# Convolution in half units at both ends of a MetaFormer kernel, with the first image's FFN spread over the second unit

## What is computed

```python
x = x + conv(ln_c(x)) + ln_c(x)        # depthwise 3x3, SAME, per channel
t = to_tokens(x)                       # (32, 112*112, 96)
h = relu(qlinear(ln_t(t), W1, b1))     # q_mul: float8 e5m2 of both operands
t = t + qlinear(h, W2, b2)             # q_acc: float16 of the sums
x = from_tokens(t)
```

## Time and profile before

| | us |
|---|---|
| median of 3 runs | 3290.78 |
| lowest, highest | 3288.11, 3294.91 |
| the profiled execution | 3289.0 |
| its span on the core (first to last instruction) | 3287.3 |

### The profile page before, as it was taken

The page is one execution under the profiler, slowest core; times in us unless marked ns, Lnnn a source line. Parts: engine busy times, 40 slices in busy tenths (PEclk is TensorE's granted clock), DMA queues, the critical chain, the costliest instruction groups (busy, mean ns, idle before and its releaser), DMA issues.

```text
span 3287.3 us, 78227 instructions
## 1 busy us (share of the span) xinstructions
PE 2986.9 (91%) x24902; PEld 2502.7 (76%) x24902; DVE 3161.5 (96%) x11557; ACT 3068.9 (93%) x7282; POOL 1922.4 (58%) x913
## 2 busy tenths in 40 slices
PE   5689999999999999999999999999999999999876
PEld 5577777777877777787777778777777877788644
DVE  8559999999999999999999999999999999999998
ACT  7779999999999999999999999999999999986666
POOL 0005666666666666666666666666666666666676
PEclk9999999999999999999999999999999999999966
DMA  7777777787777777777777778777777877766533
GB/s 222 213 206 218 226 228 226 229 232 224 232 226 229 226 229 232 225 230 228 228 226 229 232 223 231 228 228 224 231 231 225 230 227 229 226 199 179 158 118 102
DMA packets 277434, 713.58 MB, mean 217 GB/s; under 512 B 35001, under 2 KB 35106, under 8 KB 277026
## 3 DMA queue, kind: packets, MB, share of 16 engines
q1 hardware_dynamic: 271394, 694.12, 72.6%
q10 hardware_dynamic: 5632, 14.45, 1.3%
HBM read 539.84 MB, written 168.59 MB: 216 GB/s over the span
## 4 chain that ended last, share of the span: by engine, by line
DVE 52%; ACT 23%; PE 18%; issue 5%; DMA 2%; POOL 1%; DVEq 0%; SPq 0%; POOLq 0%; ACTq 0%
DVE stats L650 16%; DVE xq L687 14%; PE conv_ps L430 11%; ACT images L522 10%; DVE hid L640 9%; ACT hid L502 7%; DVE hid L645 6%; PE hid_ps L393 3%; PE y_ps L408 3%; ACT images L533 2%; DVE images L699 2%; ACT y L510 2%; DVE y L667 2%; DVE rstd L678 1%; DVE xt_ps L674 1%
## 5 line engine op out<-in xcount | busy, mean ns | idle before, releaser
L430 PE MATMUL conv_ps<-images,band_ring 112*112 112x222 f32 (+1 forms) x8928 | 1872.8, 354 | 30.2 <-DMA band_ring<-bands 29.5
L430 PEld LDWEIGHTS conv_ps<-images,band_ring 112*112 112x112 f32 x8928 | 1545.6, 177 | 177.9 <-issue 31.5
L275 POOL TENSOR_TENSOR xf<-xf,y 112x768 f32<-112x768 f32 x448 | 953.0, 2127 | 1101.1 <-DVE y L667 1101.1
L502 ACT ACTIVATE hid<-hid_ps 128x896 f16<-128x896 f32 x1344 | 1234.1, 931 | 89.6 <-PE hid_ps L393 89.6
L270 POOL TENSOR_TENSOR xf<-xf,images 112x768 f32<-112x768 f32 x448 | 982.2, 2192 | 259.7 <-ACT images L533 246.4
L522 ACT ACTIVATE images<-xn,neg_mean,rstd 112x96 f32<-112x96 f32 x2800 | 1088.1, 561 | 15.8 <-DVE neg_mean L682 11.3
L408 PEld LDWEIGHTS y_ps<-w2t,hid 128*128 128x128 f16 x10752 | 584.8, 100 | 365.8 <-ACT hid L502 194.4
L408 PE MATMUL y_ps<-w2t,hid 128*128 128x96 f16 x10752 | 668.3, 210 | 190.1 <-ACT hid L502 159.9
L687 DVE SCALAR_TENSOR_TENSOR xq<-xf,stats,xt_ps 112x96 fp8e5<-112x96 f32 x3584 | 840.5, 310 | 0.0
L393 PE MATMUL hid_ps<-xt,w1t 96*128 96x448 fp8e5 x2688 | 681.0, 363 | 16.9 <-ACT xt L494 16.9
L640 DVE TENSOR_SCALAR hid<-hid,b1q 128x896 f16<-128x896 f16 x1344 | 583.9, 466 | 12.8 <-ACT hid L502 12.3
(11 more groups left out here) (54 smaller groups left out, 763.5 us busy)
## 6 DMA issues: line engine op xcount, KB each, us to landing
band_ring<-bands SPq DMA_DIRECT2D x744, 294.0 KB, 5.1
xf<-in_x SPq DMA_DIRECT2D x462, 336.0 KB, 5.1
out<-xf SPq DMA_DIRECT2D x448, 336.0 KB, 3.9
xn<-in_x SPq DMA_DIRECT2D x434, 336.0 KB, 3.4
bands<-images ACTq DMA_DIRECT2D x16, 882.0 KB, 7.8
xf<-bands SPq DMA_DIRECT2D x24, 294.0 KB, 4.3
xf<-in_L_ffn_W SPq DMA_DIRECT2D x2, 144.0 KB, 2.8
xf<-in_L_conv_kernel SPq DMA_DIRECT2D x3, 3.4 KB
```

Source lines behind the costliest of these rows:

```text
L275: pool.tensor_tensor(res, res, y[:, e % 2], ALU.add).then_inc(summed, CW)
L430: mm = pe.matmul(dst[:, :, lo:hi], band_place(t < CONV_AT + UNIT, n)[:, PAIR * dx + i, :], images[:, m % 2, :, ch, lo + dx - 1:hi + dx - 1 ...
L502: nc.scalar.activation(hid[:, e % 2, TOK * j:TOK * (j + 1)].rearrange("p (u n) -> p u n", u=2), hid_ps[:, k, :, 0:HALF * H], ACT.Identity) ...
```

## The change

There are 17 units in place of 16: the first has image 0 alone and the last image 31 alone ("half units"), those between have images 1 and 2, 3 and 4, and so on. A half unit goes through the same 96 channels in the same 28 steps, with matmuls of 112 (or 111) moving columns in place of 224, and saves half as much for each group. Convolution begins at t = -43 (`CONV_AT`), 15 steps after the first normalisation in place of 29, and ends at t = 432.

The FFN of image 0 (chunks 0 to 13) is done in the steps -14, -12, ..., 12, during the convolution of unit 1 (images 1 and 2); from t = 14 chunk t is done in step t as before.

The banded matrices are built in three thirds of 84 larger builds, six in each step, into three separate images of the buffer `images`, in the order third 2, 0, 1. Unit 0 takes thirds 0 and 1 as weights right from where they were built and loads only third 2 (16 groups); its ring of six is gone. A normalisation that writes over a third waits until it was sent and used (`STAGED_AT`).

The first 42 chunks take moments, roots and reciprocals one step earlier (`early`), and have the ring of four and 5 columns on ACT. DVE's moments no longer wait for ACT's normalisation two chunks before; the reciprocal does.

On PE the waits of `ffn1` stand at `ffn1` itself, one for each third, no longer ahead of the matmul before it; the second third no longer waits for the first cast of its own chunk. The diff, cut to its core (that `r` and `c` are gone from all functions, with the loop that was not in use, is left out):

```diff
-FIRST_BAND_RING = 6
...
+        THIRDS = 3
+        STAGES = [(1, 1), (0, 0), (1, 0)]
+        BUILT = (2, 0, 1)
+        STAGED_AT = {CHUNKS: 2, 2 * CHUNKS: 0, 3 * CHUNKS: 1}
+        TGROUPS = GROUPS // THIRDS
+        QB = NB // THIRDS
+        def band_stage(q):
+            b, i = STAGES[q]
+            return images[:, b, i, :, :].rearrange("p c w -> p (c w)")[:, 0:QB * H] \
+                .rearrange("p (g n h) -> p g n h", g=TGROUPS, h=H)
...
+        SEND_AT = {2: (4, 1), 0: (14, 2), 1: (22, 2)}
+        STEP_SETUPS = 6
...
-        CONV_AT = -UNIT - 1
+        CONV_AT = -UNIT - 1 - CHUNKS
+        UNITS = B // IMGS + 1
+        FIRST_NORMS = UNIT + CHUNKS
...
+        def ffn(t):
+            if t < CHUNKS:
+                return [(t + CHUNKS) // 2] if t >= -CHUNKS and t % 2 == 0 else []
+            return [t] if t < TOTAL else []
...
+        def unit_images(t):
+            m = (t - CONV_AT) // UNIT
+            return slice(1, IMGS) if m == 0 else slice(0, 1) if m == UNITS - 1 else slice(0, IMGS)
...
-            return (e // UNIT) % 2, e // CHUNKS % IMGS, slice(CW * k, CW * k + CW)
+            return (e + CHUNKS) // UNIT % 2, (e // CHUNKS + 1) % IMGS, slice(CW * k, CW * k + CW)
...
+        def early(t, lag):
+            late, soon = t + lag + LOOP, t + lag + LOOP + 1
+            return [n for n in (late, soon) if 0 <= n < TOTAL and (n == soon) == (n < FIRST_NORMS)]
...
+        LOADED_FROM = 2 * TGROUPS
+        def bands_at(n):
+            if n < LOADED_FROM:
+                return band_stage(n // TGROUPS)[:, n % TGROUPS]
+            return band_ring[:, (n - LOADED_FROM) % BAND_RING]
...
-                    if e % UNIT == 0:
-                        wait(pool, conv_saved, GROUPS * (2 * r + e // UNIT + 1))
+                    if e == 0 or (e + CHUNKS) % UNIT == 0:
+                        wait(pool, conv_saved, GROUPS * ((e + CHUNKS) // UNIT + 1))
...
-                def ffn1_may_start(r, e):
-                    wait(pe, xt_copied, LOOP * r + e + 1)
-                    wait(pe, hid_cast, J * (LOOP * r + e))
-                def ffn1_may_end(r, e):
-                    wait(pe, hid_cast, J * (LOOP * r + e) + J - 2)
...
+                def ffn1(e, j):
                     k = (J * e + j) % 2
+                    if j == 0:
+                        wait(pe, xt_copied, e + 1)
+                    wait(pe, hid_cast, J * e + j - 1)
...
-                            if w == HALF - 1 and j == J - 1 and at_last:
-                                at_last()
...
-                        mm = pe.matmul(dst[:, :, lo:hi], band_place(t < CONV_AT + UNIT, n)[:, PAIR * dx + i, :],
-                                       images[:, m % 2, :, ch, lo + dx - 1:hi + dx - 1], start=(dx == 1),
+                        mm = pe.matmul(dst[:, imgs, lo:hi], bands_at(n)[:, PAIR * dx + i, :],
+                                       images[:, m % 2, imgs, ch, lo + dx - 1:hi + dx - 1], start=(dx == 1),
...
-                    for s in normed:
-                        wait(dve, s, LOOP * r + n - 1)
+                    wait(dve, normed[1], n - 1)
...
                 def invert_c(n):
+                    wait(dve, normed[0], n - 1)
```

More of the change, by code:

```diff
@@ L227, in setups, with band_arrival @@
+        def band_arrival(n):
+            return band_in[(n - LOADED_FROM) % BAND_RING], dma_count(n - LOADED_FROM, BAND_RING)
+        def setups(t):
             n = STEP_SETUPS * (t - NORM_AT)
-            return range(n, min(n + STEP_SETUPS, QUARTERS * SETUPS)) if c == t and n >= 0 else range(0)
+            return range(n, min(n + STEP_SETUPS, THIRDS * SETUPS)) if n >= 0 else range(0)
         def run(eng, step):
-            for c in range(NORM_AT - 1, LOOP_AT):
-                step(0, c, c)
@@ L233, in run @@
[L233 to L238, removed]
+            for t in range(NORM_AT - 2, END):
+                step(t)
         with nc.Block() as block:
@@ L306, in store, with load_xf @@
[L306 to L310, removed]
+                    return dram[n, :, cols, :]
+                def load_xf(e):
+                    sp.dma_start(xf[0:H, e % FFN_RING], chunk_of(x, e)).then_inc(xf_in[e % FFN_RING], 16)
+                def store(e):
+                    wait(sp, summed, CW * (e + 1))
+                    sp.dma_start(chunk_of(out, e), xf[0:H, e % FFN_RING]).then_inc(x_out[e % FFN_RING], 16)
@@ L311, in load_xn, with load_bands @@
+                def load_xn(n):
                     for s in normed:
-                        wait(sp, s, norm_place_free(r, n))
-                    sp.dma_start(norm_place(n), chunk_of(x, r, n)).then_inc(norm_arrival(r, n)[0], 16)
-                def load_bands(r, c, t):
+                        wait(sp, s, norm_place_free(n))
+                    sp.dma_start(norm_place(n), chunk_of(x, n)).then_inc(norm_arrival(n)[0], 16)
+                def load_bands(t):
                     for ch in conv_channels(t):
[L317 to L325, removed]
@@ L341, in _, with step @@
+                def step(t):
+                    for n in early(t, 3):
+                        load_xn(n)
+                    for e in ffn(t + 3):
+                        wait(sp, x_out[(e) % FFN_RING], dma_count(e - FFN_RING, FFN_RING))
+                    for e in ffn(t - 3):
+                        store(e)
+                    for e in ffn(t + 3):
+                        load_xf(e)
+                    load_bands(t + 2)
                 run(sp, step)
                 for i in range(FFN_RING):
-                    sp.wait_ge(x_out[i], dma_count(0, TOTAL - 1 - (TOTAL - 1 - i) % FFN_RING, FFN_RING))
+                    sp.wait_ge(x_out[i], dma_count(TOTAL - 1 - (TOTAL - 1 - i) % FFN_RING, FFN_RING))
@@ L491, in copy_xt @@
-                def copy_xt(r, e):
-                    wait(act, xt_mm, LOOP * r + e + 1)
+                            act.wait_ge(s, SETUPS // 2 * (BUILT.index(third) + 1))
+                    lo, hi = TGROUPS * k // SENDS, TGROUPS * (k + 1) // SENDS
+                    act.dma_start(bands[TGROUPS * third + lo:TGROUPS * third + hi].rearrange("g h n k -> h g n k"),
+                                  band_stage(third)[:, lo:hi]).then_inc(bands_out[third], 16)
+                def copy_xt(e):
+                    wait(act, xt_mm, e + 1)
@@ L574, in step @@
-                    if ffn_in(t - 1):
-                        cast_hid(r, c - 1, 1)
-                    if norm_in(t + 2):
-                        root_c(r, c + 2 + LOOP)
-                    if ffn_in(t - 1):
-                        cast_hid(r, c - 1, 2)
+                    for third, (at, every) in SEND_AT.items():
+                        k, off = divmod(t - NORM_AT - at, every)
+                        if 0 <= k < SENDS and off == 0:
+                            send(third, k)
+                    for e in ffn(t - 1):
+                        cast_hid(e, 2)
```

388 lines of the change are left out of this document (168 added, 220 removed).

## The result

| | before | after |
|---|---|---|
| median, us | 3289.45 (4 runs) | 3265.75 (4 runs) |
| lowest, highest | 3286.89, 3294.91 | 3262.9, 3270.03 |
| span of the profiled execution | 3287.3 | 3264.0 |

The ratio is 0.9927 with a 95% interval from 0.991 to 0.9944; a second set of six runs of the changed kernel gave 3267.43 us and 0.9933 (0.992 to 0.9945). The forecast was 3270 us, with a sum of 3266.3 for the span.

A forecast was written before the change was run, and what follows sets the result against it. VectorE was taken to set the full stage's pace. Head 327 + full steps 2578.7 + 93.5 + 164 + 103.1 = 3266.3 us of span, 21 under 3287.3, so 3270 us forecast; own range 3254 to 3285, overall 3238 to 3306.

The forecast's parts named there:

- Part 1: Setup until the first convolution: 3.79 us a step in place of 3.29, convolution starting at 72 us (64 to 80).
- Part 2: First half unit with normalisation, 28 steps: 3.4 us each, 95 us (80 to 120).
- Part 3: Full convolution, normalisation and every other FFN step before t = 14: TensorE leads, 29 steps of 5.5, 160 us (151 to 180).
- Part 4: Full steps: 377 at an unchanged 6.840 us, 2578.7 us, only the edited waits acting here.
- Cost and gain zero: Full steps: ffn1's changed waits free TensorE, which has spare time, so 0 us, hidden by VectorE's 100%.
- Part 5: Tail: 14 last-convolution steps at 6.68, 93.5 us; then 28 steps of FFN with half a convolution at 5.85, 164 us.
- the stall: FFN steps of the tail: add_bias slowed beside POOL's addition, 0.6 us a step; without it 5.24, 17 us less.
- A: Rival: TensorE's clock falls in the tail, mean step 7.53, +47 us, 3317 us; chance 0.13.
- C: Rival: ffn1's waits at its weight loads lift TensorE's full step to 6.96, +45 us, 3315 us; chance 0.06.
- B: Rival: the head doesn't fill, 4.0 us a step in the first half unit, 5.9 in unit 1; 3299 us; chance 0.12.
- D: Rival: the head fills better, 3.0 a step in the first half unit, 5.2 in unit 1, setup 5 less; 3245 us; chance 0.19.

The follow-up runs named there:

- the two full-width runs: Changed kernel with full-width matmuls, one image read twice, in the last half unit (3282.63 us) or the first half unit (3288.33 us).
- the repeat: The changed kernel run once more, unchanged: 3267.43 us, ratio 0.9933.
- the new place alone, at the old counts: Changed kernel with ffn1's waits still at ffn1, but asking for as many casts as the kernel before: 3272.45 us, ratio 0.9942.

## Why the prediction held

**The frame.** A step costs as much as its fullest engine, and the change exchanges 14 full steps for emptier ones that are filled: this is what the table shows, and the two full-width runs confirm that the half width carries it (by the times 15 to 17 us at the end and 21 to 23 at the beginning, depending on which set of the changed kernel they are held against). The steps of each stage, worked out from the busy times of its neighbours, were right within 6% everywhere.

**Part 1, setup**: 72 forecast, 72.6 measured. Some of this is luck: with the same setup, the first convolution starts anywhere from 69.4 to 74.1 us in the profiled executions. A copy of 384 elements took 0.54 us, 0.10 more than one of 288, as was taken; the rate of the row, which the prediction names for it, would have given 0.15. The earlier moments were costed as one step's delay of 3.79 us, and the run without them starts 2.6 us sooner; that this delay buys nothing was not asked, and the same run showed it.

**Part 2, first half unit**: 95 forecast, 90.3 measured. The bound of 0.1 us for a half matmul was the right end (0.10). DMA, at a share of 0.87 and 272 GB/s, ran as the setup's row suggested (283). The clock did fall here now and then, to 0.94 on average. It cost little: in the repeat it was 0.86 in the same window, and the last save of the half unit came at 160.76 us in place of 160.04.

**Part 3, unit 1**: 160 forecast, 168.4 measured; the mis-sized term. The share of work was nearly right (TensorE busy for 145.87 of 160 us, 5.3 a step where 5.19 was taken), the loss beside it was 9%, not 6%. The longest wait of the stage is POOL's for its chunks, 81.6 us, but POOL is busy for only 49.93 of 160 us, and the chain that ended last doesn't pass through that wait. It goes another way; pieces of it from 209 to 220 us (start, us, what):

```profile
209.20 2.35 ACT images L505 x6
...
211.56 0.32 SPq L315
...
212.86 6.46 DMA band_ring<-bands
...
219.46 1.35 PE conv_ps L419 x6
```

A load of banded matrices stands in SP's queue behind the load of a chunk for the normalisation (L315), and that one waits until ScalarE has normalised the chunk whose place it takes; then the convolution goes on when the matrices are there. Six loads of banded matrices make up 33.8 us of the chain's 160 (21.1%), and five of them come behind L315 in this way. The waits of SP's queue from 165 to 325 us (total, times, longest):

```profile
SPq L315 <- ACT images L505: 52.1, 28, 3.3
SPq L325 <- PE conv_ps L419: 40.6, 23, 4.5
SPq L195 <- DVE images L681: 24.1, 15, 4.7
```

SP stood for 117 of 160 us. That the queue is the cause of the 9% was only read from these rows, not tested: no run has the loads in another order. The term itself is known to a few us: in the executions whose heads are the same or differ in the waits alone, chunk 14's copy came at 338.1, 338.8, 339.9, 341.5, 342.0 and 345.4 us, the last with the clock down for some 30 us of the first 270.

**Part 4, full steps**: 2578.7 forecast, 2574.5 measured. "Cost and gain zero" for the waits was the step that failed. In the full stage it was nearly true, 0.006 us a step or 2 us of the 4; most of the rest lies in the first 14 full steps, which took 6.72 each, for a cause that is open. But the same edit acts in the last full convolution, where TensorE is the bound and not VectorE: there the cover named (VectorE's 100%) does not exist, and part 5 took 6.68 unchanged. It was 6.42, with 3.6 us in these 14 steps. The row that should have told was the one quoted for the opposite, TensorE waiting for ACT at L408; it was weighed against the stage with spare time alone. The same wait stands in the last convolution of the kernel before, 10.3 us from 2922 to 3102, where no other engine covers it:

```profile
PEld y_ps L408 <- ACT hid L502: 10.3, 15, 0.7
```

**Part 5, last half unit**: 164 forecast, 164.9 measured, with the clock at 1.00 to 3160 us and the stall still there: the three `add_bias` take 1.78 us, the first of them begun while POOL's addition runs, as in the earlier trace rows:

```profile
3099.29 2.19 POOL L274 TENSOR_TENSOR xf<-xf,images 112x768 f32<-112x768 f32 x1
...
3100.68 1.78 DVE L620 TENSOR_SCALAR hid<-hid,b1q 128x896 f16<-128x896 f16 x3
```

**The rivals.** A did not come: with TensorE busy for 131.72 of 157 us (84%) the clock held. C would have been the other sign of what the waits did; it did not come: with the new place alone, at the old counts, the full step is 6.831 us, and in the full stage of the changed kernel TensorE stands idle for 9.6 of 191 us where it was 11.6. B and D came in halves: part 2 better, part 3 worse by 8. So the total is as near as it is because +8 us in part 3 met -5 in part 2, -4 in the full steps and -4 in the last full convolution, the last two mostly from the waits. The kernel that keeps the old waits, and so does only what the forecast had priced, took 3273.17 us against 3270 and was in the forecast's own range too.

## What to carry to other kernels

When a pipeline's stages overlap, cost each step by its fullest engine and move work from the stage where three meet into the ends; then ask separately whether the filled ends are better than the plain ones (here the spread FFN gained nothing, and by the marks was about 4 us worse than no spread). An edit that "costs nothing because another engine is the bound" has to be priced again in every stage where that engine is not. A wait should ask for the buffer it needs and nothing more: two matmuls that may run beside a cast were worth 0.22 to 0.26 us of a 6.7 us step, in the stage in which TensorE was the bound.

## What the runs showed of the hardware

An fp32 matmul of 112 x 112 weights and 112 moving columns runs at 0.10 us an instruction, just half of the full width's 0.193; loading the weights, which is not halved, adds nothing that shows. At 84% of busy time TensorE's clock stayed at 2.4 GHz for 28 steps, where at 55% it had fallen; in the first half unit, busy for 67.82 of 85 us with waits among them, it averaged 0.94 (0.86 in the repeat), and with full-width matmuls (95.00 of 95.00 us) it held 1.00.
